# A graph layer on one core: z computed in two 64-row tiles at once, its one-hot rows made by VectorE, and three z slots of two PSUM banks

## What is computed

```
h = relu(layernorm(x))
msg_in     = concat(h[src], h[dst], edge_attr)              # 64 + 64 + 32
messages   = silu(msg_in @ W1 + b1) @ W2 + b2
att        = softmax(silu(msg_in @ Wa1 + ba1) @ Wa2 + ba2, over all edges)
aggregated = segment_sum(messages * att, dst)
out        = x + silu(concat(h, aggregated) @ Wu1 + bu1) @ Wu2 + bu2
```

## Time and profile before

| what | value |
|---|---|
| median of 3 runs | 2454.44 us (2444.82 to 2455.82) |
| the profiled execution: span from the first to the last instruction | 2482.0 us |
| busy in the span: GpSimd, TensorE, VectorE, ScalarE | 1529.9, 1101.1, 1086.6, 919.5 us |
| mean granted TensorE clock | 0.668 of full speed |
| moved by DMA | 228.43 MB, 92 GB/s over the span |

### The profile page before, as it was taken

One profiled execution on the slowest core, in us unless ns is written; L12 is line 12 of the kernel. 1 busy time (PEld: TensorE's weight loads), 2 busy tenths in 40 slices (PEclk: granted clock), 3 DMA queues, 4 the chain that ended last, 5 costly groups with the idle time before them and its releaser, 6 DMA issues.

```text
span 2482.0 us, 21022 instructions
## 1 busy us (share of the span) xinstructions
PE 1101.1 (44%) x6767; PEld 963.4 (39%) x6767; DVE 1086.6 (44%) x2367; ACT 919.5 (37%) x1107; POOL 1529.9 (62%) x1628
## 2 busy tenths in 40 slices
PE   4334444444444444444444444444444444444447
PEld 3223343444333333444333334343433333444444
DVE  4344444444444444444444444444444444444445
ACT  3333333334333333334333333343433333333433
POOL 4666666666666666666666666666666666666650
PEclk8566666666666666666666666666666666666766
DMA  7433333333333333333333333333333333333321
GB/s 202 106 90 90 90 89 88 92 91 95 98 93 88 90 88 88 90 93 90 99 95 89 89 90 89 87 94 89 98 95 91 89 90 90 87 93 90 95 65 27
DMA packets 101990, 228.43 MB, mean 92 GB/s; under 512 B 45184, under 2 KB 65460, under 8 KB 91636
## 3 DMA queue, kind: packets, MB, share of 16 engines
q1 hardware_dynamic: 47588, 120.63, 18.5%
q0 software_dynamic: 51584, 105.75, 17.2%
q10 hardware_dynamic: 2704, 0.66, 0.1%
HBM read 218.91 MB, written 8.00 MB: 91 GB/s over the span
## 4 chain that ended last, share of the span: by engine, by line
issue 48%; PE 33%; DVE 9%; another core or an unknown queue 7%; ACT 1%; SPq 1%; DVEq 0%; DMA 0%; ACTq 0%
PE bank L622 20%; PE bank L636 11%; DVE hot L865 2%; DVE v L902 2%; DVE bank L912 1%; DVE prod L895 1%; PE bank L732 1%; PE bank L722 0%; DVE lgb L921 0%; DVEq L875 0%; ACT comb L492 0%; PE bank L584 0%; ACT s L524 0%; PE bank L655 0%
## 5 line engine op out<-in xcount | busy, mean ns | idle before, releaser
L404 POOL DMA_INDIRECT p_rows<-p_tab,src_all x1612 | 1521.9, 944 | 872.3 <-issue 464.7
L622 PE MATMUL bank<-q_win,comb 128*128 128x128 f32 x3224 | 723.7, 369 | 981.9 <-issue 963.8
L622 PEld LDWEIGHTS bank<-q_win,comb 128*128 128x128 f32 x3224 | 643.9, 279 | 1099.1 <-issue 1095.4
L492 ACT ACTIVATE comb<-dst_b,row_of 96x1024 f32<-96x1024 int32 (+1 forms) x162 | 219.0, 1352 | 1336.6 <-PE bank L622 1227.8
L911 DVE TENSOR_TENSOR bank<-bank,p_rows 128x128 f32<-128x128 f32 x80 | 23.9, 299 | 1205.5 <-remote 672.6
L636 PE MATMUL bank<-hot,v 128*65 128x96 f32 x3200 | 320.1, 252 | 344.7 <-issue 274.8
L636 PEld LDWEIGHTS bank<-hot,v 128*65 128x65 f32 x3200 | 282.7, 141 | 342.1 <-issue 264.5
L912 DVE TENSOR_TENSOR bank<-bank,p_rows 128x512 f32<-128x512 f32 (+1 forms) x403 | 266.5, 666 | 71.7 <-PE bank L622 38.6
L524 ACT ACTIVATE s<-bank 128x512 f32<-128x512 f32 x403 | 232.1, 589 | 108.7 <-DVE bank L912 83.8
L498 ACT ACTIVATE comb<-comb,ones 96x1024 f32<-96x1024 f32 (+1 forms) x162 | 218.9, 1351 | 2.7
L865 DVE TENSOR_TENSOR hot<-bank,rel 128x960 f32<-128x960 f32 x162 | 178.3, 1139 | 0.0
(11 more groups left out here) (108 smaller groups left out, 304.0 us busy)
## 6 DMA issues: line engine op xcount, KB each, us to landing
dst_b<-dst_row SPq DMA_DIRECT2D x80, 960.0 KB
p_rows<-p_tab,src_all POOLq DMA_INDIRECT x1612
comb<-efT SPq DMA_DIRECT2D x80, 320.0 KB
q_win<-q_tab SPq DMA_DIRECT2D x81, 48.0 KB
p_tab<-s SPq DMA_DIRECT2D x12, 256.0 KB
q_tab<-s SPq DMA_DIRECT2D x12, 256.0 KB
out<-s SPq DMA_DIRECT2D x6, 256.0 KB, 2.3
x_sb<-x SPq DMA_DIRECT2D x2, 512.0 KB, 5.1
```

The costliest lines, as they stand in the source:

```text
L404: pool.indirect_dma_start(p_rows[:, a, t * H2:(t + 1) * H2], None, p_tab, bass.IndirectOffsetOnAxis(src_all[:, g * TG + t:g * TG + t + 1], ...
L492: nc.scalar.activation(comb[0:WIN, a, c0:c1], dst_b[:, c0:c1], ACT.Abs, bias=row_of[0:WIN, bass.ds(g, 1)]).then_inc(abs_ok, 1)
L622: last = nc.tensor.matmul(ps_z[q][:, (t % TQ) * H2:(t % TQ + 1) * H2], comb[:, a, t * P:(t + 1) * P], q_win[:, a, :], start=True, stop=True)
```

## The change

z is computed in two halves of the array. An edge quarter now has a span of QW = 32 nodes of its own, so a matmul needs 32 one-hot rows and 32 attribute rows: 64 rows. `comb` holds in partitions 0 to 63 the first two tiles of each quarter and in partitions 64 to 127 the other two, and `q_win` has the quarter's 32 nodes and the weights in both halves. There are still four matmuls for each quarter, alternately from the upper and the lower half; each half writes a bank of its own, and the two banks are a slot. There are three slots, so z(g,q) now waits until ScalarE has read the z of three quarters before. The one-hot rows are made by VectorE with one compare over all 128 partitions (`own_nodes`), which also overwrites the attribute rows, so the attributes are loaded after it. ScalarE's L492 and L498 are gone.

SyncE loads for each group 10 small windows of 32 rows, two pieces of `dst_b` (each the dst row of half the edges, broadcast to 32 partitions, 160 KB) and two attribute blocks of 160 KB.

```diff
-    WIN = P - DE
+    WIN = 96
+    QW = DE
+    HB = 2 * QW
+    QH = TQ // 2 * P
+    SLOTS = 3
-        ps_w = ps_small[:, 2 * P:2 * P + TG]
+        ps_w = ps_part[:, 2 * P:2 * P + TG]
+        def slot(g, q):
+            return z[:, (g * NQ + q) % SLOTS, :, 0:QH]
+        def load_windows(eng, g, a):
+            for q in range(quarters(g)):
+                node = eng.value_load(bases_i[0:1, bass.ds(NG + g * NQ + q, 1)], min_val=0, max_val=N - QW)
+                for h in range(2):
+                    eng.dma_start(q_win[h * HB:h * HB + QW, a, q, :], q_tab[bass.ds(node, QW), :]).then_inc(win_ld[a], 16)
...
             def load_group(g, a):
                 nxt2 = following(g)[1]
                 if nxt2 is not None:
-                    sp.wait_ge(abs_ok, 2 * g + 4)
-                    load_dst_b(sp, nxt2)
                     sp.wait_ge(z_done, (g + 1) * NQ)
+                    load_windows(sp, nxt2, a)
+                    sp.wait_ge(own_ok, g + 3)
+                    if nxt2 < LAST:
+                        load_dst_b(sp, nxt2 + 1)
                     load_ef(sp, nxt2, a, ef_ld[a])
-                    load_window(sp, nxt2, a)
...
-                        if g > 1 and t == 3 * TQ + 1:
+                        if g > 1 and t == 3 * TQ + 2:
...
-                wait(pe, silu_ok, (g - 1) * NQ + q + 1)
-                if q in (0, 2):
-                    pe.wait_ge(comb_ok, 2 * g + 1 + q // 2)
-                for t in range(q * TQ, (q + 1) * TQ):
-                    last = nc.tensor.matmul(ps_z[q][:, (t % TQ) * H2:(t % TQ + 1) * H2], comb[:, a, t * P:(t + 1) * P], q_win[:, a, :],
-                                            start=True, stop=True)
+                wait(pe, silu_ok, g * NQ + q + 1 - SLOTS)
+                out = slot(g, q)
+                for k in range(TQ // 2):
+                    for h in range(2):
+                        rows_h, cols = slice(h * HB, (h + 1) * HB), slice(q * QH + k * P, q * QH + (k + 1) * P)
+                        last = nc.tensor.matmul(out[:, h, k * H2:(k + 1) * H2], comb[rows_h, a, cols], q_win[rows_h, a, q, :], start=True, stop=True)
                 last.then_inc(z_done, 1)
...
-                for q in [q for q in (1, 2) if q in quarters]:
+                for q in [q for q in (0, 1) if q in qs]:
                     zmm(nxt, 1 - a, q)
                 if late:
                     sums(g - 1)
-                for q in [q for q in (3, 4) if q in quarters]:
+                for q in [q for q in (2, 3, 4) if q in qs]:
                     zmm(nxt, 1 - a, q)
...
+            def own_nodes(g, a):
+
+                n = quarters(g)
+                nc.vector.tensor_scalar(node_no[:, a, 0:n], base[:, NG + g * NQ:NG + g * NQ + n], row_in[:, 1:2], None, ALU.subtract).then_inc(node_ok, 1)
+                dve.wait_ge(node_ok, g + 1)
+                dve.wait_ge(dst_b_ld, 32 * (g + 1))
+                wait(dve, z_done, (g - 1) * NQ)
+                nc.vector.tensor_tensor(comb[:, a, 0:n * QH].rearrange("p (q e) -> p q e", e=QH), dst_b[:, 0:n * QH].rearrange("p (q e) -> p q e", e=QH),
+                                        node_no[:, a, 0:n].unsqueeze(2).broadcast_to([P, n, QH]), ALU.is_equal).then_inc(own_ok, 1)
...
                     one_hots(g - 1, 1)
                     weighted(g - 1, 1 - a)
+                if following(g)[1] is not None:
+                    own_nodes(g + 2, a)
```

More of the change, by code:

```diff
@@ L518, in group @@
             def group(g, a):
-                nxt2 = following(g)[1]
                 if is_last(g):
                     weights(g - 1, 1 - a)
-                for q in range(tiles(g) // TQ):
+                for q in range(quarters(g)):
                     act.wait_ge(z_ok, g * NQ + q + 1)
-                    nc.scalar.activation(silu_rows(a, q), halves(ps_z[q][:]), ACT.Silu).then_inc(silu_ok, 1)
-                    if q == 2:
-                        if g > 0 and not is_last(g):
-                            weights(g - 1, 1 - a)
-                        if nxt2 is not None:
-                            one_hot_abs(nxt2, a, 0)
-                    if q == 3 and nxt2 is not None:
-                        one_hot_relu(nxt2, a, 0)
-                    if q == 4 and nxt2 is not None:
-                        one_hot_abs(nxt2, a, 1)
-                        one_hot_relu(nxt2, a, 1)
+                    nc.scalar.activation(silu_rows(a, q), halves(slot(g, q)), ACT.Silu).then_inc(silu_ok, 1)
+                    if q == 2 and g > 0 and not is_last(g):
+                        weights(g - 1, 1 - a)
             groups(act, group)
@@ L596, in _ @@
                     pe.wait_ge(base_ok, 1)
[L597 removed]
+                    nc.tensor.matmul(ps_small[:, 0:NG + NQT], ones[0:1, :], bases_f[:], start=True, stop=True).then_inc(baseB_done, 1)
             for b in range(NB + 1):
@@ L641, in group @@
                 late = not (isinstance(g, int) and g == 0)
-                quarters = range(tiles(nxt) // TQ) if nxt is not None else []
-                for q in [q for q in (0,) if q in quarters]:
-                    zmm(nxt, 1 - a, q)
-                for q in [q for q in (1, 2) if q in quarters]:
+                qs = range(quarters(nxt)) if nxt is not None else []
+                for q in [q for q in (0, 1) if q in qs]:
                     zmm(nxt, 1 - a, q)
@@ L680, in group_any @@
                 def group_any(g):
-                    pe.wait_ge(g_ld, (g + 1) * 48)
+                    pe.wait_ge(g_ld, (g + 1) * 64)
                     T = tiles(g)
                     for q in range(T // TQ):
-                        wait(pe, g_zok, g * NQ + q - 1)
+                        wait(pe, g_th, g * NQ + q - 1)
                         pe.sem_inc(turn, 1)
-                        for t in range(q * TQ, (q + 1) * TQ):
-                            last = nc.tensor.matmul(ps_z[q % 2][:, (t % TQ) * H2:(t % TQ + 1) * H2], comb[WIN:P, 0, t * P:(t + 1) * P], q_win[WIN:P, 0, :],
-                                                    start=True, stop=True)
+                        for k in range(TQ // 2):
+                            for h in range(2):
+                                rows_h, cols = slice(h * HB + QW, (h + 1) * HB), slice(q * QH + k * P, q * QH + (k + 1) * P)
+                                last = nc.tensor.matmul(z[:, q % 2, h, k * H2:(k + 1) * H2], comb[rows_h, 0, cols], q_win[rows_h, 0, 0, :],
+                                                        start=True, stop=True)
                         last.then_inc(g_z, 1)
@@ L1154 @@
     arrays, args = {}, []
-    for name in ["x", "src", "dst", "dst_row", "efT"] + _INS[1:]:
+    for name in ["x", "src", "dst", "dst_h", "ef_h"] + _INS[1:]:
         a = np.ascontiguousarray(laid[name])
```

191 lines of the change are left out of this document (101 added, 90 removed).

## The result

The changed kernel takes 2567.07 us (median of 4 runs, 2564.89 to 2575.38); the kernel before beside it takes 2455.13 us. The ratio is 1.0477, 95% interval 1.0448 to 1.0505 (the plain quotient of the two medians is 1.0456). That is 112 us slower, where +22 was forecast.

A forecast was written before the change was run, and what follows sets the result against it. Bound: GpSimd's gathers, with one self-made 4.4 us stop each period waiting for an addition whose z signal from TensorE is held. Terms +30 - 6 - 8 + 6 = +22 us on 2482.0, 2504 profiled, 2476 us median; range 2390 to 2585.

The forecast's parts named there:

- case A: GpSimd's gathers: one stop for 20 gathers, now at tile 8 behind a full addition; 2476 us, chance 0.40.
- Rival D: GpSimd's gathers: z(g+1,1)'s signal is held too, so a stop each 16 tiles; +95 us, 2571 us, chance 0.20.
- the longer addition: At GpSimd's stop: waiting for a whole addition, 694 ns, rather than its first piece, 299 ns; +30 us over 77 stops.
- the small second stops: GpSimd's waits on L912, 22.2 us in 34, would go; -6 us.
- SyncE's queue ... Nothing.: SyncE's ten window loads a group have nearly two periods before z needs them; no cost in the steady part.
- The term on quarter 2: TensorE: z(g+1,2) moves behind the sums, its signal is held, and the stop waits for a whole addition; +30 us.
- the slow gait: While gathers follow each other, TensorE gets instructions slowly and its signals arrive once gathers stop; one 4.4 us stop a period.
- the start: 18 more window loads ahead of the first z of groups 0 and 1; +6 us, up to +76 us.
- the end: At the program's end the last additions lie behind one another as before; nothing.
- VectorE's one-hots: VectorE's compare and subtraction, 1.8 us a group, covered by its wait of 15 to 16 us; nothing, +138 us uncovered.
- the halves: TensorE's z with 64-row matmuls: a record each 0.12 us against 0.21; credited only behind stops, -8 us.
- the stops go altogether, 2123 us: GpSimd's gathers: all 76 stops of 4.36 us vanish, -331 us, 2123 us; chance 0.14.

The follow-up runs named there:

- The order alone: Kernel before with only TensorE's order changed, z(g+1,2) placed behind the sums: 2481.97 us beside 2450.35, ratio 1.0107.
- the second run: The changed kernel run again with no edit: 2637.17 us beside 2490.4 for the kernel before, ratio 1.0614.
- the last two kernels above: Changed kernel without nine of ten window loads a group from group 2 on, 2506.39 us; kernel before with z(g+1,2) behind the sums, 2481.97 us.
- a pause: Changed kernel with GpSimd waiting ahead of tile 0 until the previous group's last four gathers have landed: ratios 1.0589, 1.0579, 1.0585, without the gait.

## Why the prediction was wrong, by its steps

**Right: the place and the number of the stops.** One stop for 20 gathers, at tile 8, behind a full addition of quarter 2: 79 waits for `L936`. So the stops stand as in case A, the forecast; their length does not. Rival D gave 2571 us, close to the 2567 measured, by more stops at the old length. There are not more, they are longer; that D's number fits is chance. The stated range, 2390 to 2585 us, holds the measured time only because it was drawn wide enough for D.

**Right in size, its reason not shown: the order's own price.** The sum had +30 us for the longer addition and -6 for the small second stops. The order alone cost 2481.97 - 2450.35 = 31.6 us by the medians, and by the ratio 1.07%, some 26 us (18 to 34). The stops' totals don't show the longer addition, as said above. The -6 rests on a misreading: of the 22.2 us in 34 waits of the earlier trace rows two are at the start, 6.79 and 5.28 us, and the other 32 are 0.32 us each, no longer than the issue gap.

```profile
147.44 0.94 POOL L404 DMA_INDIRECT p_rows<-p_tab,src_all  x1 [5.28 <-DVE bank L912]
```

**Wrong: "SyncE's queue ... Nothing."** This is the step that failed. I asked only whether the loads arrive in time for z, and put what they do to the other engines while they are issued at nothing. The term on quarter 2 leaned on the same step: it took it that TensorE "gets no further" from one held quarter to the next, and so as far as before; it gets less far. The stops grow: 30.34 us a period with the ten loads, 29.41 with one. 0.93 us x 77 = some 71 us of the steady part; by the ratios it is 1.0477 - 1.0207 = 2.7 points, some 66 us, and by the quotients of the medians 58 us. Forecast: 0. What the traces show of the way: with the loads, 34 or 35 of the sums' 40 records pass before TensorE slows (29 or 31 in the second run), it then starts a record each 2.5 us, and at the release z(g+1,2) is still to do, whole or but for a record; without them all 40 pass, a record comes each 1.4 us, and z(g+1,2) is over. That the loads lengthen the stops is shown, by one run with the gait against two of the changed kernel. That it is SyncE's instructions which take from TensorE's while gathers run is my reading, argued and not shown: the loads' packets are a rival that no run excludes. And what the slow gait itself is stays open.

**About right: the start; left out: the end.** The sum had +6 us for the start. In the changed kernel's first slow stretch SyncE takes 15.48 us for six window loads, and GpSimd's first stop is 13.42 us, for the 6.79 us of before:

```profile
81.72 15.48 SPq L302 DMA_DIRECT2D q_win<-q_tab  x6
...
100.82 1.49 DVE L840 TENSOR_TENSOR comb<-dst_b,bank 128x1280 f32<-128x1280 int32 x1 [36.36 <-DMA dst_b<-dst_h]
...
104.57 0.94 POOL L437 DMA_INDIRECT p_rows<-p_tab,src_all  x1 [13.42 <-DVE z L936]
```

The first stop is 6.6 us longer, the term's size, though it came with a wait for rows of `dst_b` that I had not seen. Between the last two kernels above the start is some 10.7 us and the end 7.2 us, whose price I had put at nothing.

**Right: VectorE's one-hots in the steady part.** 1482 ns each, 120.0 us in all, and the period with them is 29.41 us against 29.38 without. That run also has the halves, so a gain of these (-8 us forecast, 0.1 us a period) could hide as much in it; the two together are nothing. The pace forecast for the halves is right: 32 records in 3.97 us behind the stop, (3.97 - 0.37) / 31 = 0.12 us each.

**The sum, redone from runs:** order 26 to 32 us, loads 58 to 71, start and end 18 to 20: 102 to 123 us for the 112 measured. The parts come from three occasions, and two of them from ratios whose intervals are 16 and 28 us wide, so that the sum closes is no test of each.

**An unstated premise.** Everything in the prediction takes the slow gait as the kernel's own. It isn't. Without it GpSimd has no stop at all, and every variant of the changed kernel without a pause lies 0.2 to 0.3% over the kernel before, at 2110 to 2116 us. The case "the stops go altogether, 2123 us" was in the prediction as something the change might bring; nearly this level came and went with no change in the program.

## What to carry to other kernels

When an engine shows idle "issue" time in long stretches, added loads from a queue that looks idle can have a price, even where the bounding path never waits for them: here nine small loads a group cost 0.93 us of a period of 30. Ask what they take while they are under way, and not only whether their result is late. Where a stop is released at a fixed delay behind the last gather (4.5 us here), what counts is the work that still stands ahead of the signal at that moment, so the signal that the bounding engine waits for is a candidate to stand earlier; with the gait that was not measured here. And profile the kernel before a second time on another occasion before you build on a stall in its trace: here 347 of 2455 us were a condition of the run.

## What the runs showed of the hardware that I had not expected

- The slow gait is there or not by occasion, for the same program on the same chip number: 2450 to 2490 us with it, 2104 to 2110 us without. Its rows: 963.8 us of TensorE's "issue" idle for z against 1.6 us.
- Two window loads of SyncE took 8.48 us at the start, six took 15.48 us; and in the steady part ten are spread over 26.38 us. Without the gait ten take 6.94 us (the kernel with the matmuls upper, upper, lower, lower):

```profile
1212.72 6.94 SPq L302 DMA_DIRECT2D q_win<-q_tab  x10
```

- From the last gather's start to TensorE's release 4.5 us pass, in the changed kernel with z still to do (1199.79 to 1204.25), in the kernel before with the new order (1196.04 to 1200.49), and without the nine loads (1207.61 to 1212.08).
- With quarter 2 behind the sums TensorE idles for `v` ahead of them (4.83 us at 1209.62 in the kernel with the order alone), and the granted clock over the sums is 0.60: 40 records in 5.75 us. In the earlier trace rows the sums followed on z with a gap of 0.24 us, at a granted clock of 1.00: 38 records in 3.50 us.
- The granted clock over the steady part is 0.59 with 64-row matmuls and 0.67 with 128-row ones (the column ahead of the DMA share in the windows above), though TensorE's busy time fell. No run tells why.
